# A four-layer kernel with six state-space scans: the beginning of each scan run written in another order

## The reference

```
# layer 1, and both directions of layer 2, per batch b (E = 512 channels, N = 16 states)
dbc   = u @ Wdbc                      # 64 columns for the step, 16 for B, 16 for C
delta = softplus(dbc[:, :64] @ Wdt + bdt)
for t in order:                       # over the 1024 tokens, backward for the second
    h = exp(delta[t] * A) * h + delta[t] * B[t] * u[t]      # h is 512 x 16
    y[t] = h @ C[t]
y = y + u * D
# layer 2
z1, z2 = (ln(x) @ Wz) @ Wc1, (ln(x) @ Wz) @ Wc2             # the inputs u of the two scans
out = silu(ln(x) @ Wx) * (ssm(z1) + flip(ssm(flip(z2))))    # the factor in front is the gate
```

## Time and profile before

| | before |
|---|---|
| median of 3 runs | 1971.57 us (1970.94 to 1975.65) |
| profiled execution | 1970.25 us, of it 1968.5 us span |
| PE busy | 1868.5 us (95%) |
| DVE busy | 1602.0 us (81%) |
| ACT busy | 1421.5 us (72%) |
| POOL busy | 1046.7 us (53%) |
| mean granted TensorE clock | 0.976 |

### The profile page before, as it was taken

How to read it: one execution, slowest core, us unless ns; L and a number is a source line. 1 busy time by engine, 2 the same in 40 slices (tenths; PEclk the granted TensorE clock), 3 DMA queues, 4 the chain that set the end, 5 groups by cost and what they waited for, 6 DMA issues and landing times. The chain is left out here.

```text
span 1968.5 us, 32685 instructions
## 1 busy us (share of the span) xinstructions
PE 1868.5 (95%) x12312; PEld 1344.0 (68%) x12312; DVE 1602.0 (81%) x2125; ACT 1421.5 (72%) x2666; POOL 1046.7 (53%) x603
## 2 busy tenths in 40 slices
PE   6989999999999999989999999989998999999997
PEld 3664899748997599869995799689974323332323
DVE  5665999668997699879995999689977989999742
ACT  3425999378992899699953999699944277777775
POOL 3031699417994299829980599469943500003000
PEclk9989899999999999999999999999999799999999
DMA  5022212102121112101110112021101111111000
GB/s 199 1 92 90 65 55 59 46 15 79 55 60 49 34 55 60 44 22 56 60 39 2 38 60 55 23 65 55 59 19 28 40 39 38 37 36 37 20 23 22
DMA packets 57548, 95.19 MB, mean 48 GB/s; under 512 B 14951, under 2 KB 23559, under 8 KB 55982
## 3 DMA queue, kind: packets, MB, share of 16 engines
q1 hardware_dynamic: 55854, 88.90, 15.2%
q0 software_dynamic: 1536, 4.20, 0.7%
HBM read 73.55 MB, written 6.91 MB: 41 GB/s over the span
## 5 line engine op out<-in xcount | busy, mean ns | idle before, releaser
L973 POOL TENSOR_TENSOR A<-A 128x1024 f32<-128x1024 f32 x384 | 895.8, 2409 | 231.9 <-ACT small L885 191.9
L893 ACT ACTIVATE A<-A,negA 128x512 f32<-128x512 f32 x768 | 549.1, 717 | 30.5 <-DVE A L954 23.7
L954 DVE TENSOR_TENSOR_SCAN A<-A,small,PS 128x512 f32<-128x512 f32 x384 | 453.8, 1257 | 8.2 <-ACT A L893 5.1
L954 DVE TENSOR_TENSOR_SCAN A<-A,PS 128x512 f32<-128x512 f32 x384 | 431.7, 1198 | 21.6 <-PE PS L806 10.9
L831 PE MATMUL PS<-ident,A 128*128 128x128 f32 x3072 | 401.9, 274 | 12.8 <-POOL A L973 9.4
L806 PE MATMUL PS<-A 128*128 128x128 f32 x3072 | 383.6, 276 | 0.3
L806 PEld LDWEIGHTS PS<-A 128*128 128x128 f32 x3072 | 362.4, 192 | 4.5 <-DVE A L954 1.3
L831 PEld LDWEIGHTS PS<-ident,A 128*128 128x128 f32 x3072 | 348.0, 141 | 20.0 <-POOL A L973 12.2
L1730 ACT ACTIVATE A<-PS 128x512 f32<-128x512 f32 x512 | 267.9, 603 | 123.6 <-PE PS L1693 123.4
L1499 DVE TENSOR_REDUCE A<-PS 128x1 f32<-128x512 f32 x512 | 319.7, 681 | 40.0 <-PE PS L1486 38.6
L870 ACT ACTIVATE A<-A,small 128x512 f32<-128x512 f32 x320 | 229.5, 717 | 14.1 <-PE PS L812 14.0
(11 more groups left out here) (194 smaller groups left out, 1837.9 us busy)
## 6 DMA issues: line engine op xcount, KB each, us to landing
A<-scrc SPq DMA_DIRECT2D x192, 256.0 KB, 3.2
A<-A SPq DMA_DIRECT2D x360, 32.0 KB
scr<-A SPq DMA_DIRECT2D x4, 1024.0 KB, 4.9
W<-in_wa SPq DMA_DIRECT2D x2, 1536.0 KB, 9.8
X<-in_x SPq DMA_DIRECT2D x4, 512.0 KB, 5.4
scr<-W SPq DMA_DIRECT2D x128, 1.5 KB
out<-X SPq DMA_DIRECT2D x4, 512.0 KB, 2.9
W<-in_w SPq DMA_DIRECT2D x1, 1984.0 KB, 7.6
```

Of the source, the lines that this page charges most:

```text
L893: e.activation(A_B[i % 4], r.DT[:, dt, ci * 512:(ci + 1) * 512], ACT.Exp, scale=negA[:, r.n, dt * 16 + s:dt * 16 + s + 1]).then_inc(*decay ...
L954: e.tensor_tensor_scan(h, a, u, init, ALU.mult, ALU.add).then_inc(*scanned.up((q, i)))
L973: e.tensor_tensor(h, h, CB[k % 2].unsqueeze(1).broadcast_to([128, 2, 512]), ALU.mult).then_inc(*weighed.up((q, pair)))
```

## The change

It rewrites the beginning of all six runs, and a little of their ends:

- `xd`, `dt` and the activations go half by half: PE makes `xd` of the first half, its four `dt`, then `xd` of the second half and its `dt`. ACT does abs and exp of the first half before it copies `xd` of the second half.
- ACT loads one function table at the start of a run (`natural_log_exp_and_others`, which holds exp, ln, abs and copy) where it loaded two or three before. The gate is written without Silu (Identity), and Silu is applied in two instructions at the run's end (`open_gates_s`), where a table load is added.
- The eight z or gate products are dealt out in five places (`PARTS`): none or two after the first `xd`, one before the second half's `dt`, three before `du` is turned, two behind the turned first half, and the last two behind the first four units on PE (`more(4)`). ACT takes the last four of them in unit 2 of its loop (`more(5)`).
- `du`'s second half is no longer turned before the units, but between them: PE turns one block after each of the units formed at i = 1 to 4 of its loop; DVE copies two of the blocks in front of its scans 4 and 5, ACT copies the other two in units 4 and 5 of its loop.
- The blocks of the first half are scaled first and copied afterwards, where each was scaled and copied in turn.
- Unit i < 4 is formed as soon as its own bank's block is copied, where all four had to be copied.
- The backward run's first `xd` is made inside the forward run's last pairs (`early`).
- The DVE extra (`meanwhile`: L1161, L1281, or the statistics) moves from in front of `delta` to behind the first half's `du`.
- SP's stream is as before, the waits for the last turned block among it.

```diff
+        def inputs_t(e, w, r, ready, more, begun=False):
+            q = r.q
+            if not begun:
+                banks.seek(4)
+                project_xd_t(e, w, r, r.order[0], ready)
+            more(0)
+            banks.seek(5)
+            project_dt_t(e, w, r, r.order[0])
+            project_xd_t(e, w, r, r.order[1], ready)
+            more(1)
+            banks.seek(3)
+            project_dt_t(e, w, r, r.order[1])
...
+            more(2)
+            banks.seek(4)
+            for j in range(4):
+                turn_du_t(e, w, r, 0, j)
+            more(3)
...
+            if not begun:
+                copy_xd_s(e, w, r, r.order[0])
+            more(0)
+            e.preload_act_table_set("natural_log_exp_and_others")
+            size(0)
+            decline(0)
+            copy_xd_s(e, w, r, r.order[1])
+            more(1)
+            size(1)
...
+            log(0)
+            decline(1)
+            log(1)
+            more(2)
...
@@ inputs_v
-            if meanwhile:
-                meanwhile()
             for p, c in enumerate(r.order):
...
+                if meanwhile and p == 0:
+                    meanwhile()
...
@@ run_t
                 form_u(i + 3)
+                if i == 0:
+                    more(4)
+                    banks.seek(0)
+                if 1 <= i < 5:
+                    turn_du_t(e, w, r, 1, i - 1)
...
                 add_up(pair)
+                if pair == PAIRS_N - 3 and early:
+                    early()
@@ run_s
-            for j in range(2, 4):
-                copy_du_s(e, w, r, 1, j)
             first_half(w, r)
...
                 if i >= 4:
                     decay(i)
+                if i == 2:
+                    more(5)
+                if i in (4, 5):
+                    copy_du_s(e, w, r, 1, i - 2)
                 if dt % 2 and i >= 5:
                     keep((i - 5) // 2)
@@ run_v
+                if i in (4, 5):
+                    copy_du_v(e, w, r, 1, i - 4)
                 w.wait_ge(*decayed.at((q, i)))
...
+        PARTS = (slice(0, 0), slice(0, 1), slice(1, 4), slice(4, 6), slice(6, 8), slice(4, 8))
```

More of the change, by code:

```diff
@@ L899, in run_s @@
                 decay(i)
[L900 to L901 removed]
+            for j in range(4):
+                if not first_state(r, j)[2]:
+                    scale_du_s(e, w, r, j)
             for j in range(4):
@@ L1224, in gates_s, with open_gates_s @@
                 banks.give(("mx", b, m, c), act.now())
+        def open_gates_s(e, w, b):
+            w.wait_ge(*act.at(("mx", b)))
+            for p, c in enumerate(runs[3 + 2 * b].order):
+                g = MX[:, :, c * 512:(c + 1) * 512]
+                e.activation(g, g, ACT.Silu).then_inc(*act.up(("gate", b, p)))
         def layer2_sp(e, w):
```

206 lines of the change are left out of this document (108 added, 98 removed).

## The result

The changed kernel takes **1992.13 us** (median of 4 runs, 1990.93 to 1995.53) against 1973.07 (1970.94 to 1975.65, 4 runs): a ratio of 1.01, 95% interval 1.0086 to 1.0114. The profiled execution took 1990.93 us, with a span of 1989.2 and a mean clock of 0.975; before it was 1970.25, 1968.5 and 0.976. The difference of the spans, 20.7 us, is what has to be found in the trace.

The account below looks back on a forecast made before the run. POOL's 64 products with C, without pause, were taken to bound each run, so their start decides. Delays of 4.2, 5.9, 4.4, 1.4, 2.1 and 1.3 sum to +19.3 us on 1970.25; forecast 1990, range 1974 to 2000.

Parts of the forecast that it names:

- What the change does to a run is what it does to the start of that product.: POOL: a run ends 149 us after its first product with C, so only that product's start matters.
- Run 3: Scan run 3: first scan 6.7 us earlier, but work before ACT's kept state makes POOL start 1.4 us later.
- charged at half clock: PE in run 3: four units after some 4 us idle take half clock, until 865.1; part of gates +1.5.
- Runs 4 and 5: POOL starts later: run 4 +2.1, like run 2 without the addition; run 5 +1.3, by a late row of C.
- Runs 0 and 1: POOL starts later: run 0 +4.2 through ACT's kept state, run 1 +5.9 through SP's late row of C.
- ACT scales the four until 206.8, copies four to 209.1, weights 210.2, diagonals 211.5: Run 0, ACT's steps behind the turned blocks, before PE forms unit 4; POOL starts at 218.8 against 214.58.
- Run 2: Scan run 2: du 2.4 us earlier, but the addition to X and PE's order delay the kept state, +4.4.
- the unknown price of the clock: PE in run 2: the clock behind 2.7 us of idle time costs between 0 and 1.5 us.
- The lead reaches POOL: Rival: POOL's start follows the first scans, 29 us earlier in all, giving 1941; chance 0.08.
- Lead and delay cancel: Rival: each run comes out at 0 to 1.4 us, no change, 1970 to 1977; chance 0.12.
- The clock stays down longer: Rival: late gate products and their like in runs 2 to 5 run at half clock, 12 us more, 2002; chance 0.08.
- What was taken as free: End of runs 3 and 5: two Silu of 1.9 us and their table load on ACT cost nothing.

Follow-up runs that it names:

- copies_behind_keep: Changed kernel, with ACT copying turned blocks 2 and 3 of du's second half behind the first kept state instead of in front of it; 1989.05 us.
- two_keeps_first: Changed kernel with copies behind both kept states, first rows of C before the weight loads, and all gate products before the first unit; 1965.33 us.
- c_row_first: Changed kernel, with SP issuing the first two rows of C of runs 1 and 5 before the wait for the last turned block and the weight load; 1977.12 us.
- no_common_table: Changed kernel without the one table set holding exp and ln: ACT makes five table loads per run instead of one; 2004.99 us.
- blocks_at_once: Changed kernel, with PE turning the four blocks of du's second half directly behind the late gate products, in front of unit 4; 1975.6 us.
- four_edits: Changed kernel with rows of C before weight loads, gate products before the first unit, blocks turned at once, additions and statistics before delta; 1961.31 us.
- all_six: Changed kernel: copies behind both kept states, rows of C before weight loads, gates before units, blocks turned at once, additions and statistics before delta; 1956.71 us.

## Why the prediction was right

1990 was forecast and 1992.13 measured, inside the range, and the sign of each run was right, though the +1.1 of runs 3 and 5 is no more than single executions differ by in one run. The steps:

- **"What the change does to a run is what it does to the start of that product."** It held for this change: lengths stayed within 0.2 us in five runs. As a rule it fell with copies_behind_keep and two_keeps_first. I had written that I would be wrong if the products showed gaps or the first product followed the first scan by under 6 us. It follows by 9.7 to 16.2. But run 5 has a gap of 1.09 us, and its length grew by 1.36, which was in no term. The gap shrank to 0.27 when the row of C came early (c_row_first), but also to 0.37 in no_common_table, where the row came late, so its cause stays open.
- **Run 3** (+1.4 forecast, +1.1 measured) holds step by step. The lead at the first scan was 7.0 us for 6.7; the kept state came 12.4 us behind the first scan, 12.7 forecast. (The prices written for ACT's last steps, from 871.05 on, give 875.05 and not 875.6 before the state is kept; added up rightly they come to the +1.1 that was measured.) The gain at `du` was 4.6 us for 4.5, and its part from the early `xd` is confirmed at 3.5. The units, charged at half clock, took 3.15 us against 1.9 at full. The statistics took DVE 3.4 us between `du`'s halves, as charged; putting them back in front saved 1.9 us in all, most of it because the units then ran at full clock.
- **Runs 4 and 5** (+2.1 and +1.3, measured +2.2 and +1.1): right. That SP's wait for the last turned block sets run 5 is shown by c_row_first, that the wait of ACT for block 2 sets run 4 by blocks_at_once.
- **Runs 0 and 1** (+4.2 and +5.9, measured +2.2 and +4.3): the right mechanism, mis-sized by 2.0 and 1.6 us. The step that failed is "ACT scales the four until 206.8, copies four to 209.1, weights 210.2, diagonals 211.5": measured, less the 1.85 us in front, these are 205.7, 207.7, 208.7 and 209.8. PE finished the weight product 1.2 us later than before instead of 1.7 and turned the blocks in 3.19 us, not 3.67, and ACT's copies take 0.5 us each when they follow one another (four in 2.05), where I had taken 0.6. The last 0.3 is PE's: a unit and a block took 1.33 us together in the trace, where I had taken 0.93 + 0.5.
- **Run 2** (+4.4, measured +6.0): the unknown price of the clock, which I had put between 0 and 1.5 us and taken at 0, came out as 1.66, a little above it: the start of run 2 came that much earlier in c_row_first. So the term was the right one, its size a matter of the execution.
- **In front of run 0**: 1.85 us that no step had. It is mostly the clock of the two executions, in code that the change doesn't touch. That the forecast missed by 2 us only is in part luck: errors of -3.6 (runs 0 and 1), +1.6 (run 2), +1.4 (run 5) and +1.85 nearly cancel.
- **The rivals.** "The lead reaches POOL" is out as a whole, but true for its one part, the early `xd`. "Lead and delay cancel" describes the starts of runs 3 and 5. "The clock stays down longer" is out: run 3's gate products took 4.09 us against 3.60 at full clock, half a us and not 3.4. The transposes in front of them ran at half clock here, but 16 such ran at 1.00 in c_row_first (1.94 us).
- **What was taken as free** was free: the two Silu and their load end at 1038.3 in run 3, before POOL's last product (1039.6), and what follows run 5 became 0.4 us longer.
- **Which part costs what.** The six runs became 18.4 us longer. Taken out of the changed kernel one at a time, the late row of C in runs 1 and 5 gives back 12.8 us, the late products on PE 9.9 in runs 2 to 5 (1.5 of it clock) and the blocks between the units 13.8. These overlap (in runs 1 and 5 the row of C waits for the last block), the row of C was late in run 1 before the change too, and the gains, 7 for the early `xd` and a part of what the tables give, stand against them. The single shares can't be added up to the total, and I don't claim to have divided it.

## What to carry to other kernels

A lead at the beginning of a stage is worth what is left of it at the engine that then runs without a pause. So follow each moved instruction to that engine, through every queue that it is moved past: here, two products, four turned blocks and two copies in front of the first kept state ate 7 us of lead, and a weight load that waited for a moved block carried the rows of C away with it. A DMA that waits for something late belongs behind the small loads that the next stage needs at once. And a stage isn't started by its first product, but when the engine no longer stops behind it: an edit that only brings the first one forward (copies_behind_keep) gains nothing, while the fastest version, with the rows of C first, the gates and blocks early and the additions in front (and that edit too), is 1.1% faster than the kernel before (0.9873 to 0.9906).

## What the runs showed of the hardware that I had not expected

- The granted clock behind one and the same idle time isn't the same from one kernel to another: 16 transposes behind 2.68 us of idle PE took 1.94, 2.61, 2.71, 3.02 and 3.40 us. 13 transposes at the end of run 3, behind 0.15 to 0.27 us of idle PE, took from 1.64 to 3.04 us. One profile gives one case of it, worth up to 1.7 us per place here. It isn't the kernel alone: ten executions of c_row_first took 1972.8 to 1982.0 us at mean granted clocks of 0.981 to 0.972.
- Where PE had idled 0.53 us or less in front of the first units of runs 2 and 3, in seven kernels, these took 1.91 or 1.94 us every time; behind 2.68 or 3.96 us of idle time they took 1.94 to 3.65.
- The way to the first `xd` of run 0, the same code in all kernels, ended between 178.4 and 184.7 us. Differences of a few us between medians of such kernels (four_edits and all_six, 4.6) need the stretches of the trace beside them.
